# Comparing the far chunks' destinations with ends copied to PSUM, and taking the check's maximum along one operand

## What is computed

```python
h = jnp.maximum(_layernorm(x, axis=-1), 0.0)
msg = jax.nn.relu(h[src] + edge_attr)
agg = jax.ops.segment_sum(msg, dst, num_segments=x.shape[0])
h = h + agg
h = jax.nn.relu(h @ W1 + b1)
return x + h @ W2 + b2
```

## Time and profile before

| | |
|---|---|
| median of 3 runs | 1407.31 us (1406.56 to 1408.48) |
| the profiled execution | 1406.28 us, of which the span is 1404.5 us |
| TensorE (PE), busy share | 97% |
| VectorE (DVE) | 86% |
| ScalarE (ACT) | 76% |
| GpSimd (POOL) | 75% |
| chain that ended last | PE 91%, DVE 5%, ACT 2%, DMA 1% |

### The profile page before, as it was taken

How to read it: one execution, slowest core, us unless ns; L and a number is a source line. 1 busy time by engine, 2 the same in 40 slices (tenths; PEclk the granted TensorE clock), 3 DMA queues, 4 the chain that set the end, 5 groups by cost and what they waited for, 6 DMA issues and landing times.

```text
span 1404.5 us, 26571 instructions
## 1 busy us (share of the span) xinstructions
PE 1367.9 (97%) x7780; PEld 710.0 (51%) x7780; DVE 1213.3 (86%) x1867; ACT 1069.0 (76%) x1166; POOL 1054.4 (75%) x1113
## 2 busy tenths in 40 slices
PE   6787999999999999999999999999999999999998
PEld 5443555555555555555555555555555555555554
DVE  7688988888888888888888888888888888888887
ACT  6685877787777877778777787787877778787773
POOL 6777777777777777777777777777777777777775
PEclk9999999999999999999999999999999999999999
DMA  7222332332332323323233232332332323323221
GB/s 255 57 58 64 87 95 72 85 89 65 94 87 71 87 67 94 87 70 92 69 87 87 70 92 65 91 91 66 94 85 69 93 65 94 86 69 94 66 83 30
DMA packets 70785, 116.54 MB, mean 83 GB/s; under 512 B 34522, under 2 KB 35950, under 8 KB 70638
## 3 DMA queue, kind: packets, MB, share of 16 engines
q1 hardware_dynamic: 34302, 76.39, 17.2%
q0 software_dynamic: 35328, 36.25, 13.3%
q10 hardware_dynamic: 1008, 2.19, 0.5%
HBM read 111.39 MB, written 3.34 MB: 82 GB/s over the span
## 4 chain that ended last, share of the span: by engine, by line
PE 91%; DVE 5%; ACT 2%; DMA 1%; issue 0%; DVEq 0%; SPq 0%; ACTq 0%
PE ps_cand L1294 88%; PE ps L421 2%; ACT keyhot L735 1%; ACT keyhot L742 1%; DVE gath L973 1%; DVE parts L1021 1%; DVE picked L966 1%; PE ps L455 1%; DVE ends L1031 1%; DVE ps_edge L1014 0%; PE ps_cand L1250 0%; PE ps L445 0%; DMA key_pair<-key_table 0%; ACT agg L715 0%; DVEq L1070 0%
## 5 line engine op out<-in xcount | busy, mean ns | idle before, releaser
L392 POOL DMA_INDIRECT gath<-h_table,idx_all x1091 | 1040.4, 954 | 333.9 <-issue 311.4
L1294 PE MATMUL ps_cand<-table_hi,keyhot 128*128 128x448 f16 x3388 | 1197.9, 354 | 20.5 <-DVE picked L966 16.6
L1294 PE MATMUL ps_cand<-table_lo,keyhot 128*128 128x448 f16 x3388 | 1197.1, 353 | 0.0
L735 ACT ACTIVATE keyhot<-key_pair,key_bias 128x512 f16<-128x512 f16 (+1 forms) x854 | 532.7, 705 | 133.3 <-PE ps_cand L1294 131.4
L1294 PEld LDWEIGHTS ps_cand<-table_hi,keyhot 128*128 128x128 f16 x3388 | 332.0, 98 | 334.3 <-issue 15.1
L1294 PEld LDWEIGHTS ps_cand<-table_lo,keyhot 128*128 128x128 f16 x3388 | 332.2, 98 | 302.3 <-issue 2.9
L742 ACT ACTIVATE keyhot<-keyhot,hot_bias 128x3584 f16<-128x3584 f16 (+1 forms) x122 | 397.4, 3258 | 4.0
L966 DVE TENSOR_TENSOR picked<-ps_cand,cand_mask 128x448 f32<-128x448 f32 x488 | 302.5, 620 | 101.2 <-PE ps_cand L1294 100.9
L973 DVE TENSOR_REDUCE gath<-picked 128x64 f32<-128x448 f32 x488 | 299.2, 613 | 4.1
L1021 DVE SCALAR_TENSOR_TENSOR parts<-ps_edge,side 128x832 f32<-128x832 f32 x242 | 235.5, 1015 | 0.0
L1031 DVE TENSOR_REDUCE ends<-parts 128x128 f32<-128x1664 f32 x122 | 229.0, 1877 | 0.0
(11 more groups left out here) (108 smaller groups left out, 185.3 us busy)
## 6 DMA issues: line engine op xcount, KB each, us to landing
edge_pair<-edges_t SPq DMA_DIRECT2D x62, 832.0 KB
gath<-h_table SPq DMA_DIRECT2D x2560, 0.2 KB
gath<-h_table,idx_all POOLq DMA_INDIRECT x1091, 2.4
key_pair<-key_table SPq DMA_DIRECT2D x61, 256.0 KB
h_table<-h_a SPq DMA_DIRECT2D x7, 224.0 KB, 2.8
part_x<-x_t SPq DMA_DIRECT2D x29, 48.0 KB
out<-part_out SPq DMA_DIRECT2D x29, 48.0 KB
x_c<-x_cols ACTq DMA_DIRECT2D x4, 256.0 KB, 4.9
```

What stands on the lines that cost most here:

```text
L392: nc.gpsimd.indirect_dma_start(out=rows[:, r, :], out_offset=None, in_=h_table, in_offset=bass.IndirectOffsetOnAxis(ap=idx[:, r:r + 1], ax ...
L735: last = nc.scalar.activation(keyhot[u % 2][:, a, 0:n], key[u][:, P * PE_MAX - n:], ACT.Abs, bias=key_bias[:, a:a + 1])
L1294: last = nc.tensor.matmul(bank[:, 0:D * CAND], keyhot[u % 2][:, a, i * P:(i + 1) * P], half[:, a, :, :].rearrange("p d b -> p (d b)"), sta ...
```

## The change

Three edits. For the far chunks, the partition's end (first or last destination of each chunk, 112 values) is first copied into PSUM as float32, and the comparison takes its second operand from there; so each of the two comparisons becomes a copy, a wait for it, and a comparison. The near chunks keep `sides`. The maximum of both sides, an elementwise operation on two operands of 1612 values each, becomes a reduction over pairs: one operand of 3224 values, ordered so that the two sides of an edge follow each other. The PSUM place is in `ps1`, behind the 192 columns that the dense layers use.

```diff
+FAR = N_CHUNKS - 3 * SLOTS
...
+        far_ends = [ps[1][:, PART + k * FAR:PART + (k + 1) * FAR] for k in range(ENDS)]
...
+            def far_sides(k):
+
+                r = k * (TILES_PER_CHUNK - 1)
+                then(nc.vector.tensor_copy(far_ends[k], dst_i[:, FAR_CHUNKS, r]))
+                then(nc.vector.tensor_tensor(side[:, FAR_CHUNKS, k, :], dst_i[:, FAR_CHUNKS, :],
+                                             far_ends[k].unsqueeze(2).to_broadcast([P, FAR, TILES_PER_CHUNK]),
+                                             ALU.is_equal))
+
...
             def covered_edges():
-                then(nc.vector.tensor_tensor(stray[:, :, :], side[:, :, 0, :], side[:, :, 1, :], ALU.max))
+                then(nc.vector.tensor_reduce(stray[:, :, :], side.rearrange("p c k r -> p c r k"), AX_X, ALU.max))
...
                 if u < ENDS:
-                    sides(FAR_CHUNKS, u)
+                    far_sides(u)
```

## The result

| | before | after |
|---|---|---|
| median of 17 runs each, on the same chip | 1406.46 us (1405.66 to 1408.48) | 1409.41 us (1408.07 to 1413.2) |
| ratio, with its 95% interval | | 1.0022 (1.0015 to 1.0029) |
| the profiled execution | 1406.28 us, span 1404.5 us | 1413.2 us, span 1411.4 us |

The change makes the kernel 2.95 us slower, 0.22%, clear of the scatter. The profiled execution is the longest of the 17, so its end can't be read as typical; its first 150 us can.

The account below looks back on a forecast made before the run. VectorE up to 131 us, then TensorE, was taken to bound the kernel. Copies 0.52, comparisons 0 and maximum 1.66 made 2.18 us, so 1407.31 + 2.2 = 1409.5 us (+0.16%), range 1407.5 to 1411.2 us.

Parts of the forecast that it names:

- The path: VectorE's almost unbroken stretch up to 131 us: any delay between 82 and 131 us moves everything behind it.
- The copies: Casts ahead of the two far-chunk comparisons: 2 x 0.26 = 0.52 us more on VectorE, bounds 0 to 1.04.
- The comparisons: Two far-chunk comparisons with one operand in PSUM: no change from 1.67 us, within 0.01 us each way per operation.
- The maximum: The check's maximum as a reduction over 3224 elements: 3.49 us in place of 1.83, 1.66 us more.
- The two bounds: Reduction: no loss if pairs go through at once (chance 0.08); 1.68 us on top if every result costs (0.08).
- The sum on VectorE: Copies, comparisons and maximum in VectorE's early stretch: 0.52 + 0 + 1.66 = 2.18 us, with no idle time to swallow it.
- The clock: Rival: TensorE's slow phase after its pause lengthens; if doubled, 1.1 us more, 1410.6 us; chance 0.12.
- POOL's gain and its loss: Three stretched gathers become ordinary, freeing 3.83 us; POOL waits some 4.0 us at chunk 10, leaving it 0.7 us later.
- reserve of 2.0 us: At chunk 10's first candidate tile: ready about 131.5 us, needed by POOL at 133.49 us.
- Even if it were kept it would not show: At the tail, POOL's gain would not shorten the time: TensorE's line would end 2.2 us later anyway.
- POOL's line decides: Rival: gathers are what ends last, so 3.83 us less, 1403.5 us; chance 0.04.
- The 141.8 us for chunk 9's candidates: TensorE starts the first candidates of chunk 9 at 141.8 us, where it was 139.63.

Follow-up runs that it names:

- e3: Kernel before with the minimum over all edges taken twice, 1.87 us more of VectorE: 1408.30 us, ratio 1.0010 to the kernel before.
- e4: The changed kernel run again for a second profile, nothing else altered: 1409.21 us, ratio 1.0020 to the kernel before.
- e1: Changed kernel with the maximum left elementwise, so only the copies and PSUM comparisons: 1407.08 against 1406.65 us for the kernel before, ratio 1.0004.
- e2: Kernel before with only the maximum made a reduction over pairs: 1407.92 us, ratio 1.0009 to the kernel before.
- e9: The changed kernel again, on a third chip: 1412.91 against 1410.90 us for the kernel before, ratio 1.0018.
- e12: Changed kernel with 65 additional unread matmuls in TensorE's pause ahead of turn 2, third chip: 1411.06 us, ratio 1.0002 to the kernel before.
- e10: Changed kernel without POOL's waits for candidates inside a chunk, third chip: 1410.17 us, ratio 0.9997 to the kernel before.
- e5: Kernel before with the check moved from turn 1 to turns 8 and 9, second chip: 1408.57 against 1410.86 us, ratio 0.9983.

## Why the prediction was right, point by point

**The path.** That VectorE's stretch up to 131 us is handed on in full stands: in e3's profile TensorE's line is later by what was added, and the rest of the span is the same 1254.2 us in the seven profiles that end on TensorE.

**The copies.** Forecast 0.52 us, measured 0.70 (0.31 and 0.39). The cast behind the one-hot took 0.35 us, and its wait comes on top; the row of 124 values had been without the stride.

**The comparisons.** Forecast no change. The second takes 1.67 us as before; the first takes 1.67 where it took 1.60, in every profile of either kind, which is more than the bound of 0.01 us. In the kernel before it starts 0.07 us ahead of the end of a MEMSET; whether that or the operand's place makes the difference, no run tells.
The Trainium skill's table (VectorE: DVE Perf Modes, section on the TRN2 errata) had 62 cycles more for a source in PSUM, an estimate of 0.13 us for both. The trace doesn't agree on the second comparison, whose other source is in SBUF (1.67 and 1.67 us); the 0.07 us of the first would fit it.

**The maximum.** Forecast 3.49 us, measured 3.63; by its successor's start it costs 1.80 us more and not 1.66. The two bounds (0 and 3.3 us) are both excluded.

**The sum on VectorE.** Forecast 2.18 us, measured 2.73 to 2.82 in three profiles. The copies (0.70), the first comparison (0.07) and the maximum (1.80) make 2.57. The rest is one gap, ahead of L949, which is 0.18 us longer than before (0.23 in e4). It stands in every profile that has the copies and the check in its old place, e1 included, and in none of e2, e3 and the kernel before; its cause is open. The prediction had no term for it.

**The clock.** This rival, priced at up to 1.1 us with a chance of 0.12, came true in part: 14 slow matmuls in place of 7 in two of three profiles, 0.9 and 1.0 us, and nothing in the third (8 slow ones). It was mis-sized in its chance, not in its mechanism; the point from which it decides, slightly above the 7 of the kernel before, was right.

**POOL's gain and its loss.** That the 3.8 us would be freed and all given back at chunk 10 is what the profiles show. The size was off: waits of 7.8, 6.9 and 4.4 us and not 4, and POOL 0.6 to 1.6 us later than before and not 0.7. Two steps of the working made this. The waits differ because POOL's arrival was taken from one profile, and it varies: 129.4 us by the working, 126.9, 128.2 and 129.7 us in the three profiles of the changed kernel. The lateness differs because of the reserve of 2.0 us at the first tile: it was taken to the end of the tile's last matmul, but POOL's gather starts 0.9 to 1.0 us after the following matmul does (in e1, e2, e4, e9, e12 and the first profile). In the kernel before that matmul starts at 131.33 us, so POOL could have gone at 132.3 and not at 131.5, and the reserve was 1.2 us. With it the sizes come out: 2.75 of VectorE, less 1.2, plus 1.2 of additional slow phase in the very tile POOL waits for, makes 2.7 us later against VectorE (first profile: 134.69 - 80.55 against 133.49 - 82.09), and 1.6 in e9, where the slow phase is as short as before.
The Trainium skill (SBUF — State Buffer, section Who interferes with whom) infers that an operation with two SBUF inputs would leave descriptor generation alone; it also says that such an operation contends with a GpSimd instruction that reads SBUF. The traces don't agree with the first: beside the comparisons the gathers went back from 2.36 and 1.79 to 0.95 us once one operand lay in PSUM, and e1 and e2 show each hold leave with its own operation. The copy has also turned that operand from int32 into float32, but the maximum, float32 throughout, held its gather as well (2.50 us).

**"Even if it were kept it would not show."** This step failed for part of the executions. It rested on a single profile at POOL's faster pace. At the slower one the changed kernel ended on POOL (first profile, e12), and then POOL's time does count: e10, which gives back part of the gain, is 2.7 us below e9. The rival "POOL's line decides" had a chance of 0.04 because it was asked only whether VectorE had time to spare. But POOL's line was only some 0.9 us from being the last, less than the 2.4 us between its two paces; the 0.1 us named in the expectation of e5 is not what the rows give. It didn't turn the sign, since POOL's line, too, became later.

**The total.** 1409.5 us forecast, 1409.41 measured, but this is luck, two errors that cancel: the difference was 2.95 us and not 2.2, and the median of the kernel before, in these 17 runs, 1406.46 us and not the 1407.31 of the three shown. Of the ratio I expected 1.0016; it is 1.0022, with 1.0016 inside the interval. The 141.8 us for chunk 9's candidates (141.73 in the first profile) came out by luck too: 2.7 us of VectorE and 0.9 of the clock, less 1.5 ahead of the edits. How the 2.95 us of the medians divide among VectorE (2.8), the clock (0 to 1.0), POOL and the final store can't be told from single profiles.

## What to carry to other kernels

A hold of one engine by another is worth removing only on the line that ends last; here POOL was freed of 3.8 us, and the price, 2.8 us on VectorE, was paid in a stretch in which VectorE had no room. The same edits, with the check moved to turns in which VectorE waits anyway, made the kernel 0.4% faster than before: place first, then price. And where two lines end within 1 us of each other, ask of every edit what it does to both, and don't take the order of the two from one profile.

## What was not expected of the hardware

- POOL issues indirect gathers at one of two steady paces, 1.249 or 1.251 us, which differ between executions and hold from chunk 10 to the end; over 1010 gathers it makes 2.4 us. In e10, at the slower pace, TensorE's rest was the same 1254.2 us as at the faster one.
- After pauses of about the same length, TensorE was slow for different numbers of matmuls: 14, 14, 8 and 8 behind 8.0 to 8.1 us (first profile, e4, e9, e10), 13 behind 6.2 (e1), 10 behind 7.1 (e2), 8 behind 7.2 (e3), 7 behind 7.0 (before). The length of the pause doesn't tell the length of the slow phase.
- A reduction over pairs with a result for every second element runs nearly at the rate of reductions over 7 and 13 elements: 3.63 us for 3224 elements, where that rate gives 3.49.
- An elementwise operation with both operands in SBUF held a gather that overlapped it: 2.36, 1.79 and 2.50 us in place of 0.94. The same work as a reduction of one operand, or with one operand in PSUM, held none (0.95 and 0.96 us).
